# Language-model tower on one core: bias add, low parts and the squares in another order on GpSimd and ScalarE

## The reference

```python
h = weight[words] * keep_mask[words]                     # gathered embedding rows
n = layernorm(h)
u, res = split(n @ in_proj_w.T)                          # 512 and 256 channels
u = causal_conv(u, conv_w, 4 taps) + conv_b              # per channel
delta = softplus(u @ dt_proj_w.T + dt_proj_b)
g = u * sigmoid(delta)
state = 0.9 * state + 0.1 * g                            # scan over the tokens
h = h + state @ out_proj_w.T + res
x = layernorm(h)
xq, wq = blockwise 6-bit float quantisation of x and ffn_w, blocks of 32, dequantised
out = h + xq @ wq.T + ffn_bias
```

## Time and profile before

| | |
|---|---|
| time, median of 3 runs | 1024.26 us (1023.52 to 1025.87) |
| profiled execution | 1026.02 us, span 1024.2 us |
| mean granted clock of PE | 0.988 of full speed |
| PE busy | 955.7 us, 93% |
| PE weight loads busy | 781.8 us, 76% |
| DVE busy | 829.8 us, 81% |
| POOL busy | 750.3 us, 73% |
| ACT busy | 647.2 us, 63% |

### The profile page before, as it was taken

One profiled execution on the slowest core, in us unless ns is written; L12 is line 12 of the kernel. 1 busy time (PEld: TensorE's weight loads), 2 busy tenths in 40 slices (PEclk: granted clock), 3 DMA queues, 4 the chain that ended last, 5 costly groups with the idle time before them and its releaser, 6 DMA issues.

```text
span 1024.2 us, 14964 instructions
## 1 busy us (share of the span) xinstructions
PE 955.7 (93%) x4892; PEld 781.8 (76%) x4892; DVE 829.8 (81%) x1218; ACT 647.2 (63%) x1342; POOL 750.3 (73%) x749
## 2 busy tenths in 40 slices
PE   2689999999999999999999999999999999999996
PEld 1476887777877778787777788777878787878885
DVE  4767988888888888898888888888889878889866
ACT  5755666666667766666676666766666666665541
POOL 6647777777787777878777788777787787776652
PEclk9889999999999999999999999999999999999998
DMA  5213432244433234443223443323444322343101
GB/s 170 69 35 103 123 91 81 88 115 124 124 103 95 77 93 123 123 123 102 77 88 103 123 123 108 94 76 91 123 123 123 102 68 88 112 124 103 62 23 42
DMA packets 73790, 100.81 MB, mean 98 GB/s; under 512 B 12577, under 2 KB 61089, under 8 KB 73761
## 3 DMA queue, kind: packets, MB, share of 16 engines
q1 hardware_dynamic: 67616, 83.59, 25.7%
q0 software_dynamic: 6144, 16.85, 7.2%
HBM read 51.65 MB, written 48.76 MB: 98 GB/s over the span
## 4 chain that ended last, share of the span: by engine, by line
POOL 41%; issue 21%; DVE 20%; PE 9%; ACT 7%; DMA 1%; POOLq 0%; DVEq 0%; ACTq 0%
POOL g_lo L381 16%; POOL rows L366 11%; DVE u L757 10%; POOL xT_lo L430 5%; ACT n L558 4%; DVE h L767 3%; DVE stats L773 3%; POOL rstd L415 3%; POOL h L425 3%; ACT u L515 2%; PE psZ L1074 1%; PE psZ L1068 1%; PE psZ L1067 1%; POOL nmr L419 1%; POOL u_lo L388 1%
## 5 line engine op out<-in xcount | busy, mean ns | idle before, releaser
L757 DVE SCALAR_TENSOR_TENSOR u<-psU,cw,u 128x511 f32<-128x511 f32 x378 | 260.0, 741 | 82.6 <-ACT u L515 80.2
L388 POOL TENSOR_TENSOR u_lo<-u,u_hi 128x512 fp32r<-128x512 f32 x128 | 164.5, 1296 | 83.1 <-ACT u_hi L522 79.0
L1074 PE MATMUL psZ<-u_lo,dt_hi 128*128 128x512 f32 x512 | 208.9, 408 | 12.5 <-POOL u_lo L388 12.5
L381 POOL TENSOR_TENSOR g_lo<-g,g_hi 128x512 fp32r<-128x512 f32 x128 | 199.8, 1580 | 20.6 <-ACT g_hi L533 19.9
L1067 PE MATMUL psZ<-u_hi,dt_hi 128*128 128x512 f32 x512 | 201.4, 393 | 5.7 <-ACT u_hi L522 4.6
L1068 PE MATMUL psZ<-u_hi,dt_lo 128*128 128x512 f32 x512 | 202.2, 395 | 0.0
L522 ACT ACTIVATE u_hi<-u 128x512 fp32r<-128x512 f32 x128 | 81.0, 633 | 138.4 <-DVE u L757 137.7
L366 POOL DMA_INDIRECT rows<-table,ids x128 | 127.1, 993 | 44.9 <-issue 44.1
L1074 PEld LDWEIGHTS psZ<-u_lo,dt_hi 128*128 128x128 f32 x512 | 96.5, 188 | 58.9 <-POOL u_lo L388 40.7
L515 ACT ACTIVATE u<-psU,cb,cw 128x512 f32<-128x512 f32 x126 | 94.3, 772 | 39.7 <-PE psU L1010 39.6
L533 ACT ACTIVATE g_hi<-g 128x512 fp32r<-128x512 f32 x128 | 76.6, 621 | 62.3 <-DVE g L837 62.3
(11 more groups left out here) (120 smaller groups left out, 2215.5 us busy)
## 6 DMA issues: line engine op xcount, KB each, us to landing
turned_n<-nb_blocks SPq DMA_DIRECT2D x31, 512.0 KB
nT<-turned_n SPq DMA_DIRECT2D x124, 128.0 KB
out<-h SPq DMA_DIRECT2D x31, 512.0 KB, 4.6
turned<-xb SPq DMA_DIRECT2D x30, 512.0 KB, 2.6
xT<-turned SPq DMA_DIRECT2D x120, 128.0 KB, 2.9
rows<-table,ids POOLq DMA_INDIRECT x128
dt_stage<-dt_wT SPq DMA_DIRECT2D x1, 1024.0 KB, 5.8
g<-in_wT SPq DMA_DIRECT2D x1, 768.0 KB
```

The costliest lines, as they stand in the source:

```text
L381: pool.tensor_tensor(g_lo[:, m, :], g[:, m, :], f32(g_hi[:, m, :]), ALU.subtract).then_inc(g_lo_ready[m], 1)
L388: pool.tensor_tensor(u_lo[:, m, :], u[:, m, :], f32(u_hi[:, m, :]), ALU.subtract).then_inc(u_lo_ready[m], 1)
L757: dve.scalar_tensor_tensor(u[:, m, back:T], u_psum_tile(st, m)[:, 0:T - back], cw[:, m, TAPS - 1 - back:TAPS - back], u[:, m, back:T], ALU ...
L1074: ins = pe.matmul(psZ[:, m % 2, :], dt_hi[:, k, o], u_lo[:, k, :], start=False, stop=(k == M - 1))
```

## The change

On POOL, the low part of g's last block goes ahead of the bias add; the low parts of u 0 and 1 go ahead of mean1; the low part of xT goes ahead of the low parts of u 2 and 3; variance1 and inverse_root1 go behind the low parts of u 2 and 3. On ACT, the high part of xT goes ahead of first_tap(2), (3), and both go ahead of square1_rows. No instruction is added, removed or resized, and DVE's, PE's and SP's orders stay.

```diff
@@ -450,24 +450,24 @@
                     mean1(2)
                     return
 
+                if st.back:
+                    split_g(M - 1, s - 1)
                 if st.tail:
                     add_bias()
-                if st.back:
-                    split_g(M - 1, s - 1)
                 if st.first:
                     variance1(1)
                     inverse_root1(1)
-                if st.early:
-                    mean1(2)
                 split_u(0)
                 split_u(1)
                 if st.early:
+                    mean1(2)
+                if st.tail:
+                    split_xT()
+                split_u(2)
+                split_u(3)
+                if st.early:
                     variance1(2)
                     inverse_root1(2)
-                split_u(2)
-                split_u(3)
-                if st.tail:
-                    split_xT()
                 if st.gather:
                     ring, turn = st.ring(3)
                     pool.wait_ge(ids_loaded[ring], 16 * turn)
@@ -642,12 +642,13 @@
                     normalise1(1)
                 if st.early:
                     mask_rows(2)
-                    square1_rows(2)
+                if st.tail:
+                    split_xT()
                 if not st.first:
                     first_tap(2)
                     first_tap(3)
-                if st.tail:
-                    split_xT()
+                if st.early:
+                    square1_rows(2)
                 split_u(2)
                 split_u(3)
                 if st.early:
```

## The result

The changed kernel takes 1060.87 us (median of 3 runs, 1060.68 to 1062.63) against 1024.26: a ratio of 1.036, 95% interval 1.0334 to 1.0385. The forecast was slower, 1033 us, in a range of 1021 to 1043. The direction held, the size did not: 36.6 us, of which 8.6 were forecast.

A forecast was written before the change was run, and what follows sets the result against it. The prediction took a loop through every engine to bound the kernel, replaced by one through inverse_root1 and normalise1: 30.15 + 0.4 for a collision = 30.55 us against 30.23, over 27 intervals +8.6 us, so 1033 us, range 1021 to 1043.

The forecast's parts named there:

- The bound, and what the change removes: A 30.2 us loop through every engine bounds full steps; mean1, squares and xT_lo leave it, and both PE stalls go.
- The second loop, 30.15 us: From add_linear through u_hi, u_lo 3, inverse_root1, normalise1, turn_n1 and gate(1) back: becomes the longest, 30.15 us a step.
- The loads of xT: Ahead of xT_hi on ACT: the four loads land in time, cost taken as 0, upper bound 0.44 us.
- D: Rival: xT's loads land behind mask_rows, holding ACT and the taps; 12 us more, 1045 us; chance 0.06.
- g_lo 0 starts at 1.55 after the next X: On POOL, inverse_root2 moves earlier, so g_lo 0 starts 1.55 us after the next X instead of 3.8.
- X: The start of add_linear (L830) on DVE, from which places in a step are counted.
- Moved by another 0.08, that is 0.4 a step.: Collision of POOL's g_lo 0, 1 with DVE's L806, taken from the late step: 0.4 us a step.
- the upper bound, 0.9: Most the collision could cost a step: L806 waits out both g_lo subtractions, with nothing given back behind it.
- The late step: Step of the kernel before with g_lo 0, 1 at 1.47 after X: L806 takes 1.80 us, median 1.23.
- The sum: Full step: 30.15 + 0.4 = 30.55 us against 30.23, so +0.32 x 27 = +8.6 us.
- B: Rival: same second loop without the collision, 30.15 us a step, 1022 to 1024 us; chance 0.15.
- C: Rival: stalls' removal counts and PE paces, 974 us, if normalise1 is done 1.8 us sooner; chance 0.12.

The follow-up runs named there:

- the run without any meeting: Changed kernel, with GpSimd waiting for the dequantise (xd_ready) ahead of the low part of g 0: 1022.90 us, ratio 0.996.
- pair behind a wait: Kernel before, two gathers moved behind the low parts of g 0 and 1, and g_lo 0 also waiting for g_hi 1: 1045.91 us, ratio 1.020.
- behind block_max: Changed kernel, with GpSimd waiting for block_max (amax_ready) ahead of the low part of g 0: 1041.10 us, ratio 1.015.
- GpSimd's half alone: Kernel before with only GpSimd's reordering from the diff, ScalarE's order as before: 1120.38 us, ratio 1.093.
- ScalarE's half alone: Kernel before with only xT_hi and the taps ahead of the squares on ScalarE, GpSimd's order as before: 1018.47 us, ratio 0.993.

## Why the prediction was wrong in its size

- **The bound, and what the change removes.** Right in the main. Both waits of PE left their places, and PE did not come to pace the step. But only the wait at linear went; that for u_lo came back at u_lo 3, as 0.46 us.
- **The second loop, 30.15 us.** Right to 0.2: the links behind u_hi 0 measured 18.52 for 18.36, ACT waits 2.95 us ahead of normalise1, DVE 2.58 ahead of turn_n1, PE 1.00 behind gate(0). Moving inverse_root1 back ahead takes the step to PE's 28.44, and that is shown by experiment, not argued.
- **The loads of xT.** Right: ACT had no wait for them (xT_hi straight behind mask_rows, 3.17 after u_hi 0). D did not occur.
- **g_lo 0 starts at 1.55 after the next X.** Right: 1.58.
- **"Moved by another 0.08, that is 0.4 a step."** This is the step that failed. The term measured 13.01 - 11.79 = 1.22 us, or 1.6 against the run without any meeting, and even the upper bound, 0.9, was too low. The late step has its pair 0.11 us earlier. There the scale came 0.91 us into the pair and was let in behind the first g_lo (0.43 us in all), so round_to_grid met the second. In the changed kernel it came 0.79 us into the pair and was held for both. The prediction looked for the price at round_to_grid alone and drew a straight line through one row; the bound should have been the whole pair falling on the first of VectorE's instructions that GpSimd can hold. It starts about 0.8 into the pair, so 2.55 - 0.8 = 1.75, an estimate; the scale took 1.81 - 0.18 = 1.63 more.

  At the place where the prediction looked it was nearly right: with the scale off VectorE, the meeting with round_to_grid costs 0.55. But the scale was held first. The scale is not an instruction with two SBUF tensor inputs. It is a tensor_scalar on SBUF in float32, and the Trainium skill has that too: in the page VectorE: DVE Perf Modes, section The perf-mode tier table, such an operation runs at 2x, and by the section Mode 2×_2P that mode uses both read ports for one tensor; GPSIMD Engine Reference, Specifications, which the prediction cited, names this mode beside the two inputs. The trace agrees: 1.81 us against 0.18 to 0.2 for 32 elements, while block_max, one instruction earlier and beside the first g_lo from 524.51 on, took the same 1.21 as in the run with the pair behind the dequantise. The half of the rule that the prediction left out was the half that decided.

  The Trainium skill also says (SBUF — State Buffer, section SBUF: two separate sides) that whoever starts first keeps the shared ports for the whole of its instruction. For one GpSimd instruction the runs agree: where the second g_lo was made to wait, the scale took 0.56 us, until the first had ended.
- **The sum.** 27 x 1.32 = 35.6 of the 36.6 us; 27 x (1.22 - 0.4) = 22 us of the miss of 28 are the collision, 27 x 0.2 = 5 the small excess of the other links over 30.15. The range was also too narrow for the prediction's own bounds: a collision of 0.9 gives 31.05 us a step and 1046 us, above the 1043 at which the range ends.
- **Rivals.** B's step without the collision was put at 30.15; the run without any took 29.95. C needed normalise1 1.8 us sooner, and the version that gives it that is the fastest one (normalise1 at 503.74, 22.0 after its X at 481.73, instead of 25.8).

What stays open: why the pair runs through whole in the changed kernel, where the scale could start 0.79 us into it (525.30 - 524.51), while VectorE gets in after the first one when it asks 0.58 (pair behind a wait), 0.63 (behind block_max), 0.91 (late step) or 1.0 to 1.1 us into it (24 of 27 steps with two gathers moved). In the changed kernel the pair runs straight behind a gather with everything ready, in the next two cases behind a pause of GpSimd; but in the last it ran straight behind a gather too. Nor does it help VectorE to ask ahead of the pair. In the one step of the changed kernel with a late gather, the scale starts at 840.42, beside the last gather (840.11 + 0.95) and 0.66 us before the pair (841.08 + 2.55), and yet takes 3.26 us: both g_lo run first. What the Trainium skill says there (SBUF — State Buffer, section SBUF: two separate sides) is on one instruction, and says nothing of which engine gets the ports at its end. A rule that fits all of these cases was not found.

## What to carry to other kernels

When an instruction is moved out of a waiting engine's way, price what moves with it: here four gathers and two subtractions of GpSimd, none of them in the diff, came 2.3 us earlier in VectorE's step (g_lo 0 at 1.58 after X instead of 3.85), and the subtractions met its scale. Where GpSimd and VectorE meet, list every VectorE instruction in that stretch that GpSimd can hold, small ones first, and bound the cost by the whole run of GpSimd instructions that are ready at once. And a small computation that feeds a long chain (here 1.6 us of inverse_root1) goes ahead of large independent ones as soon as its inputs are there: here that edit alone was worth 1060.87 - 981.77 = 79 us, the meeting that it moved away included.

## What the runs showed of the hardware

- In the changed kernel a 128x32 tensor_scalar of VectorE, 0.18 us without GpSimd in its way, took 1.80 to 1.82 in 26 of the 27 full steps and 3.26 in the other, ending 0.05 us after a pair of GpSimd subtractions of 2.55 us.
- A dequantise of 1.22 us took 5.11 and 7.44 in single steps in which three or four GpSimd instructions were ready in a row. In the second of them VectorE was shut out for 6.2 us.
- It works the other way too: a GpSimd gather that normally takes 0.95 took 1.22 where it began inside VectorE's nT_lo, and a GpSimd multiplication of four elements 1.20 instead of 0.20 beside nT_lo in the run with inverse_root1 ahead.
- PE's mean granted clock in the profiled executions was 0.967 in the slowest kernel, GpSimd's half alone, and 0.988 to 0.993 in all others. Over the full steps it was 1.00 (2.4 GHz), but for GpSimd's half alone (0.95 in the step shown) and for the step of ScalarE's half alone that is shown (0.95).
